# Dividing the later rotation tables of an attention kernel over four iterations

## What is computed

```
om = jnp.concatenate([omega, -omega], axis=-1)
ang = t[:, None, None] * om[None]
phase = jax.lax.complex(jnp.cos(ang), jnp.sin(ang))
qr = q * phase[None]
kr = k * phase[None]
s = jnp.einsum('bihd,bjhd->bhij', qr, jnp.conj(kr)).real
logits = coef * jnp.log1p(maha / nu) - 0.5 * DH_ * jnp.log(V)
A = jax.nn.softmax(logits, axis=-1)
```

## Time and profile before

| what | value |
|---|---|
| median of 3 runs | 1909.14 us (1903.48 to 1909.46) |
| the profiled execution | 1910.13 us, span 1908.3 us, mean granted clock 0.981 |
| busy share of the span | PE 94%, PEld 77%, DVE 84%, ACT 82%, POOL 76% |
| chain that ended last, by engine | PE 62%, DVE 10%, POOL 6%, issue 5%, ACT 2% |

### The profile page before, as it was taken

One profiled execution on the slowest core, in us unless ns is written; L12 is line 12 of the kernel. 1 busy time (PEld: TensorE's weight loads), 2 busy tenths in 40 slices (PEclk: granted clock), 3 DMA queues, 4 the chain that ended last, 5 costly groups with the idle time before them and its releaser, 6 DMA issues.

```text
span 1908.3 us, 40882 instructions
## 1 busy us (share of the span) xinstructions
PE 1799.2 (94%) x10660; PEld 1477.1 (77%) x10660; DVE 1611.6 (84%) x3845; ACT 1574.3 (82%) x3217; POOL 1455.2 (76%) x1289
## 2 busy tenths in 40 slices
PE   3689999999999999999999999999999999998997
PEld 2478788887888787887888778888888788876876
DVE  6888898888888887888888878888888888895884
ACT  4599888898888887888889878888888888885654
POOL 3667788888888887888888878888888888862663
PEclk8799999999999999999999999999999999998998
DMA  6132110231123101311112112310131111110111
GB/s 193 72 115 100 62 33 35 78 94 46 45 78 94 44 25 47 110 61 46 45 69 81 46 47 78 91 37 34 45 111 45 46 45 45 37 41 12 45 45 44
DMA packets 61038, 117.70 MB, mean 62 GB/s; under 512 B 13440, under 2 KB 42880, under 8 KB 52656
## 3 DMA queue, kind: packets, MB, share of 16 engines
q1 hardware_dynamic: 59888, 115.51, 18.0%
q10 hardware_dynamic: 960, 0.00, 0.0%
HBM read 99.64 MB, written 21.36 MB: 63 GB/s over the span
## 4 chain that ended last, share of the span: by engine, by line
PE 62%; DVE 10%; POOL 6%; issue 5%; ACT 2%; DVEq 0%; POOLq 0%; ACTq 0%
PE pa L757 13%; PE ps L797 11%; PE py L821 11%; PE po L832 9%; PE pp L787 7%; PE pp L809 5%; POOL qk L588 4%; PE pa L768 3%; PE pa L776 2%; DVE lg L1535 2%; DVE stats L1573 1%; DVE lg L1543 1%; DVE ps L1524 1%; DVE acc L1595 1%; POOL ek L598 1%
## 5 line engine op out<-in xcount | busy, mean ns | idle before, releaser
L588 POOL TENSOR_TENSOR qk<-rm 64x512 f32<-64x512 f32 x512 | 694.3, 1356 | 102.9 <-PE ps L797 43.7
L598 POOL TENSOR_TENSOR ek<-tabs,kn 128x512 f32<-128x512 f32 (+3 forms) x512 | 461.8, 909 | 153.5 <-DVE lg L1535 116.7
L1543 DVE CUSTOM_DVE_ANT_0 lg<-lg,tabs,ncog 128x512 f32<-128x512 f32 (+3 forms) x512 | 443.8, 885 | 0.0
L757 PE MATMUL pa<-xt,wt 128*128 128x512 f32 x1488 | 425.3, 422 | 15.3 <-issue 13.2
L797 PE MATMUL ps<-qk 128*128 128x512 f32 (+3 forms) x1024 | 376.3, 451 | 27.1 <-DVE lg L1535 25.0
L1424 DVE TENSOR_TENSOR rm<-pa,tabs 128x512 f32<-128x512 f32 x512 | 333.0, 678 | 79.4 <-POOL qk L588 71.6
L1535 DVE CUSTOM_DVE_ANT_0 lg<-ps,ek,qb 128x512 f32<-128x512 f32 (+3 forms) x512 | 279.5, 546 | 124.7 <-POOL ek L598 81.2
L821 PE MATMUL py<-pt,vt 128*128 128x128 f32 x2560 | 348.4, 275 | 0.1
L821 PEld LDWEIGHTS py<-pt,vt 128*128 128x128 f32 x2560 | 331.6, 192 | 16.3 <-issue 0.3
L757 PEld LDWEIGHTS pa<-xt,wt 128*128 128x128 f32 x1488 | 276.2, 193 | 69.1 <-issue 17.7
L1134 ACT ACTIVATE lg<-lg,qb 128x512 f32<-128x512 f32 (+3 forms) x512 | 278.3, 558 | 20.8 <-DVE lg L1535 17.5
(11 more groups left out here) (185 smaller groups left out, 2218.7 us busy)
## 6 DMA issues: line engine op xcount, KB each, us to landing
xt<-xs_d SPq DMA_DIRECT2D x56, 1024.0 KB, 4.8
tabs<-vec_d SPq DMA_DIRECT2D x8, 1536.0 KB, 8.7
xs_d<-xt SPq DMA_DIRECT2D x6, 1024.0 KB, 4.1
wt<-wraw_d SPq DMA_DIRECT2D x7, 768.0 KB, 5.8
acc<-in_L_attn_x SPq DMA_DIRECT2D x8, 512.0 KB, 7.4
tabs<-in_L_attn_x SPq DMA_DIRECT2D x8, 512.0 KB, 4.7
out<-tabs SPq DMA_DIRECT2D x8, 512.0 KB, 3.1
tabs<-rope_d SPq DMA_DIRECT2D x56, 64.0 KB, 4.3
```

The source lines that it names most:

```text
L588: pool.tensor_tensor(qk[part * DH:(part + 1) * DH, z * HH + hh, :], rm[row, 2 * part, :], rm[row, 2 * part + 1, :], ALU.add if part else A ...
L598: pool.tensor_tensor(ek[:, n % 2, 0:w], tab(par, hh, E2_T, w), kn[:, hh, 0:w], ALU.mult).then_inc(ek_pool, 1)
L757: last = mm(pa[r][:, :], wproj(par, z, kt, a, r * P, (r + 1) * P), xbuf[x][:, kt, b, :], start=(n == 0), stop=(n == 3 * KT - 1))
L1543: dve.tensor_tensor_reduce(lg[:, hh, at(n)], lg[:, hh, at(n)], tab(par, hh, T3_T, w), ncog[:, par, 0, hh:hh + 1], 3e38, ALU.add, ALU.min, ...
```

## The change

The tables are still made by the same instructions. What moves:

- `x_stats(2)` leaves the prologue and takes the place of `x_stats(3)` in iteration 0; `x_stats(3)` goes to iteration 1. `x_rstd` and `x_move` follow one iteration behind each other.
- `rope_angle(1)`, `(2)`, `(3)` go from the block in iteration 0 to the same place in iterations 1, 2 and 3; `rope_trig(k)` goes to the same place in iteration k.
- SP stores table k in iteration k, and loads group 1's decay and rotation tables in iteration 4 rather than 2 and 3.
- The buffers change: positions stay in `ang3`, and angles 1 to 3 use two planes of `tabs[1]`, the absolute value in place.

```diff
@@ sync engine @@
-                if t == 0:
-                    for k in range(ROPES):
-                        rope_store(k)
+                if t < ROPES:
+                    rope_store(t)
...
-                if t == 2:
+                if t == 3:
+                    load_weights(1)
+                if t == 4:
                     for k in range(ROPES):
                         sp.wait_ge(rope_out[k], 48)
                     load_decay(1, 1)
-                if t == 3:
                     load_rope(1, 1)
-                    load_weights(1)
@@ gpsimd, end of body @@
-                if it.own == 1:
-                    x_rstd(2)
-                    x_rstd(3)
+                if it.own in (1, 2):
+                    x_rstd(it.own + 1)
@@ scalar: rope_trig, and its place in body @@
             def rope_trig(k):
                 act.wait_ge(rope_dve, 5 * (k + 2))
-                if k == 3:
-                    act.wait_ge(rope_out[0], 48)
+                if k >= 2:
+                    act.wait_ge(rope_out[k - 2], 48)
...
-                if it.own == 1:
-                    for k in range(ROPES):
-                        rope_trig(k)
-                    act.wait_ge(rope_act, 4 * ROPES + 3)
+                if it.own is not None and it.own <= ROPES:
+                    rope_trig(it.own - 1)
+                    act.wait_ge(rope_act, 4 * it.own + 3)
                 log(c, 1, 3, it.slot)
@@ vector: rope_angle, body, prologue @@
-                if k == 1:
-                    dve.wait_ge(rope_act, 3)
-                if k == 2:
-                    dve.wait_ge(ffn_tr, 9)
+                if k >= 2:
+                    dve.wait_ge(rope_act, 4 * k + 3)
...
-                if it.own == 2:
-                    x_move(2)
-                    x_move(3)
+                if it.own in (2, 3):
+                    x_move(it.own)
...
-                if it.own == 1:
-                    x_stats(3)
-                    rope_angle(1)
-                    rope_angle(2)
-                    rope_angle(3)
+                if it.own in (1, 2):
+                    x_stats(it.own + 1)
+                if it.own in (2, 3, 4):
+                    rope_angle(it.own - 1)
                 if old:
                     add_output(cp, it.b_before, it.over, 0, 1)
...
             rope_angle(0)
-            x_stats(2)
             dve.wait_ge(grp[0], 16 * TABLE_LOADS)
```

More of the change, by code:

```diff
@@ L140, in build @@
         stage = qk[:, 0:3, :].rearrange("p a n -> p (a n)").rearrange("p (q r) -> p q r", r=W2)
-        tokens, turns = wot[:, 1, :], yt[:, 0, :]
-        abs_ang = pt[:, 1, :]
-        spare = vt[:, :, :, :].rearrange("p a j n -> p (a j n)")
-        ang = [pt[:, 0, :], yt[:, 1, :], spare[:, 2 * N:3 * N], ang3[:, :], yt[:, 1, :]]
-        rope_cs = [tabs[1][:, 0, :], tabs[1][:, 3, :], tabs[1][:, 6, :], tabs[1][:, 0, :]]
-        rope_sp = [tabs[1][:, 1, :], tabs[1][:, 4, :], tabs[1][:, 7, :], tabs[1][:, 1, :]]
-        rope_sn = [tabs[1][:, 2, :], tabs[1][:, 5, :], spare[:, 3 * N:4 * N], tabs[1][:, 2, :]]
+        tokens, turns = ang3[:, :], [yt[:, 0, :]] + [tabs[1][:, 6, :]] * 3 + [yt[:, 0, :]]
+        abs_ang = [pt[:, 1, :]] + [tabs[1][:, 7, :]] * 3 + [pt[:, 1, :]]
+        ang = [pt[:, 0, :]] + [tabs[1][:, 7, :]] * 3 + [yt[:, 1, :]]
+        rope_cs, rope_sp, rope_sn = [[tabs[1][:, 3 * (k % 2) + m, :] for k in range(ROPES)] for m in range(3)]
         xbuf = [xt[0][:, :, :, :], xt[1][:, :, :, :], hx[:, :, :].rearrange("p (k s) n -> p k s n", k=KT)]
@@ L1066, in group_trig @@
                 act.activation(ropet(0, 1), ang[-1], ACT.Sin).then_inc(rope_act, 1)
-                act.activation(abs_ang, ang[-1], ACT.Abs).then_inc(rope_act, 1)
+                act.activation(abs_ang[-1], ang[-1], ACT.Abs).then_inc(rope_act, 1)
                 act.wait_ge(rope_act, 2)
-                act.activation(ropet(0, 0), abs_ang, ACT.Sin, bias=half_pi[:, :], scale=-1.0).then_inc(rope_act, 1)
+                act.activation(ropet(0, 0), abs_ang[-1], ACT.Sin, bias=half_pi[:, :], scale=-1.0).then_inc(rope_act, 1)
             def rope_trig(k):
                 act.wait_ge(rope_dve, 5 * (k + 2))
-                if k == 3:
-                    act.wait_ge(rope_out[0], 48)
+                if k >= 2:
+                    act.wait_ge(rope_out[k - 2], 48)
                 act.activation(rope_sp[k], ang[k], ACT.Sin).then_inc(rope_act, 1)
                 act.activation(rope_sn[k], ang[k], ACT.Sin, scale=-1.0).then_inc(rope_act, 1)
-                act.wait_ge(rope_act, 4 * k + 3)
-                act.activation(abs_ang, ang[k], ACT.Abs).then_inc(rope_act, 1)
+                act.wait_ge(rope_act, 4 * k + 5)
+                act.activation(abs_ang[k], ang[k], ACT.Abs).then_inc(rope_act, 1)
                 act.wait_ge(rope_act, 4 * k + 6)
-                act.activation(rope_cs[k], abs_ang, ACT.Sin, bias=half_pi[:, :], scale=-1.0).then_inc(rope_act, 1)
+                act.activation(rope_cs[k], abs_ang[k], ACT.Sin, bias=half_pi[:, :], scale=-1.0).then_inc(rope_act, 1)
             def x_normal(n):
@@ L1253, in body @@
                     keep_turned(cp, 1, 3)
-                if it.own == 2:
-                    act.wait_ge(rope_out[2], 48)
                 exp(c, 0, 0)
@@ L1399, in rope_angle @@
                 z = ang[k]
-                if k == 1:
-                    dve.wait_ge(rope_act, 3)
-                if k == 2:
-                    dve.wait_ge(ffn_tr, 9)
+                if k >= 2:
+                    dve.wait_ge(rope_act, 4 * k + 3)
                 q = k % (ROPES + 1)
-                rope_step(ts(turns, tokens, om2[:, q:q + 1], MAGIC, ALU.mult, ALU.add))
-                rope_step(ts(turns, turns, MAGIC, -TURN, ALU.subtract, ALU.mult))
-                rope_step(stt(z, tokens, om[:, q:q + 1], turns, ALU.mult, ALU.add))
-                rope_step(stt(z, turns, REST / TURN, z, ALU.mult, ALU.add))
+                rope_step(ts(turns[k], tokens, om2[:, q:q + 1], MAGIC, ALU.mult, ALU.add))
+                rope_step(ts(turns[k], turns[k], MAGIC, -TURN, ALU.subtract, ALU.mult))
+                rope_step(stt(z, tokens, om[:, q:q + 1], turns[k], ALU.mult, ALU.add))
+                rope_step(stt(z, turns[k], REST / TURN, z, ALU.mult, ALU.add))
                 rope_step(ts(z, z, 3.1415925, -3.1415925, ALU.min, ALU.max))
```

## The result

| kernel | median | executions | ratio to before (95% interval) |
|---|---|---|---|
| before | 1909.46 us | 7, 1903.48 to 1912.49 | |
| after | 1918.45 us | 7, 1916.03 to 1923.65 | 1.0052 (1.0036 to 1.0068) |

What follows compares the result with a forecast made beforehand. PE was taken as busiest (26.52 of 27.40 us an iteration), with DVE ending its waits in the prologue and iteration 0. -4.0 - 7.4 + 7.0 + 4.9 + 4.9 + 4.5 = +9.9 us gave 1919 us; range 1908 to 1925.

Steps and rivals of the forecast that it cites:

- prologue, `x_stats(2)` gone: End of the prologue: 3.5 us leave DVE and PE's idle 3.69 us shrinks by as much; -4.0 us, ends -3.5 and -5.2.
- iteration 0, ACT ends the wait: Iteration 0: three angles (9.8 us) leave DVE, but ACT's copy then releases PE's `turn`; -7.4 us.
- iteration 1, statistics and angle: Before `add_output` in iteration 1: `x_stats(3)` and an angle, together 7.4 us less 0.4 slack, stall PE; +7.0 us.
- iterations 2 and 3, one angle each: Before `add_output` in iterations 2 and 3: an angle of 5.3 us less 0.4 slack stalls PE; +4.9 us each.
- clock behind three stalls: After the stalls of iterations 1 to 3: PE falls to its lower clock, 1.5 us each; +4.5 us, ends 0 and 7.5.
- ACT, POOL, SP: ACT's 3.6 us in iterations 1 to 3 hidden by the stall, POOL's moved root in time, SP's transfers covered; nothing.
- Rival 3: Iterations 1 to 3: the iteration's idle time absorbs the new work; -5.5 us, 1903.6 us; chance 0.10.
- the taking of turns: Angle in iteration 2: DVE and POOL alternate, one tensor instruction each, so it takes 5.3 us.
- Rival 2: Iterations 1 to 3: POOL yields and an angle costs 2.96 us everywhere; about +1.4 us, 1910.5 us; chance 0.17.
- ACT's cover: Iteration 2: ACT's copy is done at 162.3, PE reaches its `turn` at 163.8; 1.5 us over.

Runs made afterwards that it cites:

- short_trig: After with ACT's part of tables 1 to 3 cut to 8 columns and to copies, so no added table load there: 1919.89 us, 1.0052 to before.
- both_stats_in_gap: Before with `x_stats(2)` and `x_stats(3)` both moved into DVE's idle 5.89 us in the prologue: 1907.52 us, 0.9981 to before.
- short_angle: After with the angles 2 and 3 computed on 8 of 512 columns on DVE: 1922.72 us, 1.0057 to before.
- tables_only: After with the statistics of x put back at their old places, so that only the tables are divided: 1919.85 us, 1.0046 to before.
- one_input: After with the five instructions of angles 2 and 3 each replaced by a `bn_stats` with one input, on 420 columns: 1919.83 us, 1.0051 to before.
- stats_only: Before with only the statistics moved to their new places, one iteration later, tables as before: 1910.76 us, 1.0004 to before.

## Why the prediction was right, step by step

| term | forecast | measured, in the profile of after |
|---|---|---|
| prologue, `x_stats(2)` gone | -4.0 | -3.55 |
| iteration 0, ACT ends the wait | -7.4 | -7.2 |
| iteration 1, statistics and angle | +7.0 | 7.05 idle |
| iterations 2 and 3, one angle each | +4.9 each | 4.58 idle each |
| clock behind three stalls | +4.5 (0 to 7.5) | 4.2 + 1.6 + 1.7 = 7.5 |
| ACT, POOL, SP | 0 | 0 (short_trig for ACT; the steps of the ruler leave nothing for the others) |
| sum | +9.9 | +13.0 in the profile, +9.0 by medians |

**Right.** That ACT and not DVE would end iteration 0's wait: PE's `turn` names ACT's copy as its releaser, and both_stats_in_gap shows the same limit from the other side. That PE's work can't be made up behind `add_output`: the stalls came at 7.05 and 4.58 us, released by `acc`, and moving the angle behind that instruction gave 7.4 us back by the medians. Rival 3, by which the iteration's idle time absorbs the angle, falls with it.

**Right in the price, coarse in its mechanism.** The angle in iteration 2 took 4.9 us (151.68 to 156.58) where the taking of turns gave 5.3: two instructions were stretched, the second and the fourth. The Trainium skill, "SBUF — State Buffer", section "Who interferes with whom", has the shared port held for a whole instruction; the trace agrees more sharply than I had used it, with 1.26 us for an instruction of 8 columns where another takes 0.17. My expectation for short_angle priced the instructions by their size, and that was the mistake there. Rival 2 (POOL yields) falls: 4.9 and not 2.96 us.

**The mis-sized term is the clock.** "I take 1.5 us each" was 1.6 and 1.7 behind the stalls of 4.58 us but 4.2 behind the one of 7.05, where PE was at half speed for over 8 us; my reason that slowed matmuls wait for DVE anyway did not hold there, as PE is busy for all of it. The sum of 7.5 is the upper end that I gave. Nor is a longer stall simply the dearer one: in tables_only a stall of 4.58 us cost 4.2 more in iteration 1, and in short_trig the one of 7.05 cost 2.0 and those of 4.58 2.1 each, 6.1 in all.

Without the clock the forecast's sum was 5.4 and the measured one is 5.5, but here two misses of 0.6 and 0.7 us cancel (shorter stalls, smaller gains). A smaller miss beside it: PE's first score did not run at full speed (1.19 us, as before) though its idle time was gone, hence -3.55 and not -4.0.

**Luck in the number.** The median came out at +9.0, close to +9.9, while the terms of the profile add up to +13.0. Up to iteration 4, the only two profiles with after's three stalls stand at +13.0 (after) and +11.1 (short_trig), both over the forecast. What brings the median down to 9.0 is not seen in any trace; the executions differ by some 7 us in the part that the change does not touch. So the causes, the signs and the prices of the stalls were right; that the total is right within 1 us is not evidence for the 4.5.

**Right, with room.** ACT's cover was put at 1.5 us. In iteration 2 ACT's copy for PE ran from 161.39 to 161.97, and PE came to its `turn` at 165.51, 3.5 us later. It is more than I had, since ACT's load began at 155.91, before the angle was done, and PE was slower behind its stall. For the switch the Trainium skill, "ScalarE: Activation LUTs", section "What ACT_TABLE_LOAD costs", counts 2.66 us; here a load and the start of the next activation are 1.29 us apart (90.94 to 92.23 in ACT's iteration 0 of after), right behind the activation before it, and leaving the loads out won nothing.

```profile
90.20 0.72 ACT L1075 ACTIVATE tabs<-pt,half_pi 128x512 f32<-128x512 f32 x1
90.94 1.28 ACT L1129 ACT_TABLE_LOAD   x1
```

**Open.** What sets the length of the slow stretch. What the profiles show, by the ruler (one iteration of before is 27.4 us):

| idle time of PE | lost behind it, us (profile, iteration) |
|---|---|
| 7.05 | 4.2 (after, 1), 4.0 (short_angle, 1), 4.2 (one_input, 1), 2.0 (short_trig, 1) |
| 4.58 | 4.2 (tables_only, 1), 1.6 and 1.7 (after and tables_only, 2 and 3), 2.1 and 2.1 (short_trig, 2 and 3) |
| 3.15 | 4.2 (stats_only, 1), 3.3 and 3.3 (short_angle, 2 and 3) |
| 2.82 | 3.3 (one_input, 2), 0.05 (one_input, 3) |

The same idle time before the same matmuls cost different amounts, even within one execution. What decides between them was not found.

## What to carry to other kernels

Work taken off a path is worth what the next engine in line allows, and put back elsewhere it costs its full length wherever it stands ahead of an instruction that a bottleneck engine waits for: here 0.4 us of slack against 3 to 7 us of work. So look for the instruction that releases the bottleneck and put the new work behind it (here 7.4 us by the medians), or into an idle time that exists already and that the trace shows with its length (5.9 us, of which 4.4 were used). An idle time of PE has to be priced with the half-speed stretch that may follow it: behind those of 2.8 to 7.1 us here, from nothing to 4.2 us. Where one profile is compared with another, read the difference at the end of the stretch that the change touches, and take the medians of many executions for the whole.

## What the runs showed of the chip that I had not expected

- A DVE `TENSOR_SCALAR` on 8 columns beside a POOL tensor instruction takes 1.18 to 1.26 us, where another angle instruction on 8 columns takes 0.17: making such an instruction smaller hardly helps, making them fewer should (this was not tried). `BATCH_NORM_STATS2` is not stretched (0.62 us for 420 columns, five in a row).
- The slow stretch of the clock isn't ordered by the idle time ahead of it (table above).
- In the thirteen profiles the part from iteration 4 on, the same work on the engines in all, took 1695 to 1697 us or 1701 to 1704, whatever stood ahead of it.
- Idle products of constants held the clock (1.10 us instead of 2.05 for the projection behind them) where they ended before the wait did.
- ACT's table load ran inside the semaphore wait of the activation that needs it.
